# Macaron block on one core: a later state's product ahead of the product with C, softmax steps one at a time, four B/C buffers

## The chip, the cores and the metric

One core of one Trainium2 chip. The metric is the device time of one execution in microseconds (us). Shown are the median of three runs and one profiled execution.

## The reference, cut to what matters

The input is 4 sequences of 1024 rows by 128 features. Three blocks follow each other, each on a layer-normed input and with a residual:

- **Expert block**, used twice, scaled by 0.5: 8 experts, `silu(x @ w_gate[e]) * (x @ w_up[e])` (128 to 512), then `@ w_down[e]` (512 to 128). The experts are summed with weights `cw`: a softmax over 8 router logits times a softmax over 8 gating logits divided by 0.1, divided by its own sum.
- **Mamba block** between them: `x @ W_in` gives `xs` and `z` of 256 channels each; a causal convolution of 4 taps and silu give `xc`; `xc @ W_x` gives 64 rows for `dt` and 16 rows each of B and C. For each of 16 states n: `h = exp(dt*A[n]) * h + (dt*xc) * B[n]`, a scan over 1024 steps, and `y += h * C[n]`. Then `y + D*xc`, times `silu(z)`, `@ W_out`.

## The kernel before, in words

The work is cut into tiles of 512 rows, 8 tiles in all. A tile goes once through the first expert block (kind 0), through mamba, and once through the second expert block (kind 1). The 16 expert passes are *positions*, in the order of `ORDER` (line 35); the last is tile 7 of kind 1. A position has 32 *slots*, one for each expert and group of 128 hidden columns. In each slot TensorE makes six matmuls for gate and up (line 643, 644, 646) and four for the down product (L700, eight records); ScalarE takes the silu of the gate (L1016); VectorE multiplies it by up (L825, the step `first`). After the fourth slot of an expert VectorE weighs the expert's output (L818, step `acc`) and GpSimd's queue adds it to the tile in memory by an accumulating DMA (L1120).

Mamba's states run beside that. For each tile and state n there are: a load of the B and C rows, broadcast to all partitions, into one of `BR` = 3 buffers BCB (L620, SyncE's queue); the product with B, step `s_b` (L912); two scans, `s_scan` j = 0 and 1 (L923); the product with C, step `s_hc` (L931, in place in one of `HR` = 4 buffers HS); two accumulating DMAs Y<-HS (L1137, GpSimd's queue). Each of these DMAs waits until the one of the state before has landed. ScalarE makes the decays (L1085). A tile is closed by `s_yz` (L945, VectorE), `s_out` (L730, TensorE) and `s_add` (L950, VectorE). Then its layer norm can start: ScalarE (L974, L982), GpSimd (L1106 to L1110), ScalarE (L988), four transposes on TensorE (L658), the high and low parts XH (L996 ScalarE, L883 VectorE), and the logits (L666).

The softmax of a position runs on VectorE in ten small instructions, each needing the one before: four (L775, L777, L779, L781; step `p_max`), then the exponentials on ScalarE (L1009, L1010), then six (L786 to L800; steps `p_norm`, `p_sum`, `p_cw`).

**The order of all instructions is made by a planner**, `timetable()` (lines 53 to 422). It is one list of steps; each engine runs its own steps of that list in order and waits on semaphores. The planner keeps a clock for each engine ("pe", "v", "a", "p"), adds a written cost for each step, and lets *streams* (prep, tail, before, scans, closing) give out steps between slots. `side()` gives the streams a turn, three times in a slot; a stream that yields True goes on at once, one that yields False waits for its next turn. `fill(at)` gives out scan steps while VectorE's clock is under a mark 3 us ahead of TensorE's, less 1.0. `finish(k)` drives a stream to its end and adds 0.3 us to TensorE's clock each time round, giving out no slot; it is called for the softmax (`prep`) before the first `acc` of a position, at the position's slot 5. At slot `LATE` = 26 of a position the planner waits in the same way, where the tile of the next position has not yet left mamba. The next position's inputs are forced by slot 29. A state's steps come from `scans(t)` (lines 256 to 290).

The written costs of VectorE's steps are the planner's only knowledge of durations: 1.17 for `s_b` and `s_hc`, 1.22 for a scan, 0.61 for a `first`, 1.0 + 0.4 + 0.3 + 0.35 for the softmax.

Of the kernel before, what the change touches and what calls it, by code (L numbers as in the profile page):

```python
# [20 lines left out]
NS = 16  # L21
# [6 lines left out]
NG = AHEAD + 1  # L28
NB = 4 - NG
HR = 4  # L30
BR = 3
EPS_LN = 1e-5
EPS_CW = 1e-9

# [2 lines left out]
ENDS = (0, NPOS - 1)  # L37
# [15 lines left out]
def timetable():  # L53
# [2 lines left out]


    steps = []
    clock = {"pe": 0.0, "v": 0.0, "a": 0.0, "p": 0.0}
    free = [(0.0, b, None) for b in range(NB)]  # L60

    def step(*what, after=0.0, **work):

        steps.append(what)
        for e, c in work.items():
            clock[e] = max(clock[e], after) + c
            after = clock[e] + SIGNAL[e]
        return after
# [5 lines left out]
    def until(at):  # L74
        while clock["pe"] < at:
            yield False

    def until_v(at):
        while max(clock["v"], clock["pe"]) < at:
            yield False  # L80
# [18 lines left out]
    def norm(b, what):  # L99
        while ln["lock"]:  # L100
            yield False
        ln["lock"] = True
        q = norms[0]
        norms[0] += 1
        yield from rows_of_x()
        yield from calm()
        if q == 0:
            at = step("ln_first", b, what, after=4.0, v=1.5, p=1.2)
            yield "first"
            at = step("ln_first_x", b, after=at, v=.7, a=.9)  # L110
        else:
            at = step("ln_sum", q, b, xn["by"], what, after=clock["pe"], a=1.6)
            yield True
            yield from calm()
            at = step("ln_square", q, b, after=at, a=1.6, p=2.0)
            yield from until(at + .3)
            at = step("ln_x", q, b, after=at, a=1.5)
        ln["lock"] = False
        yield from until(at + 0.7)
        bk = yield from take()  # L120
        at = step("ln_t", q, bk, pe=.6)
        xn.update(by=("m_tr", q + 1), lock=False)
        return q, bk[0], at

    def prep(p):
        kind, t = ORDER[p]
        q, b, at = yield from norm(t % XR, ("x", t) if kind == 0 else ("x2", t))
        at = step("p_xh", p, q, b, after=at, a=.52)
        yield from until_v(at + LATEST)
        at = step("p_xl", p, b, after=at, v=.61)  # L130
        give(b, "v_xl", p + 1, at)
        inputs.add(p)
        yield "inputs"
        yield from until(at)
        bk = yield from take()
        at = step("p_logits", p, bk, pe=.55, a=1.2)
        give(bk[0], "a_lr", p + 1, at)
        yield "logits"
        yield from until_v(at)
        at = step("p_max", p, bk[0], after=at, v=1.0)  # L140
        yield True
        if p == 0:
            yield from until(at + FIRST)
        yield from calm()
        at = step("p_exp", p, after=at, a=3.0)
        yield from until_v(at)
        at = step("p_norm", p, after=at, v=.4)
        yield True
        step("p_sum", p, v=.3)
        yield True  # L150
        step("p_cw", p, v=.35)

    def weigh(g):
        if g % E < E - 1 or g // E not in ENDS:
# [101 lines left out]
    def scans(t):  # L256
        def enter(n):
            step("s_b", t, n, v=1.17)

        bc_loads(t * NS + BR)  # L260
        for n in range(2):
            enter(n)
            yield True
        for n in range(NS):
            m = t * NS + n
            if decayed[0] <= m:
                decays(must=True)
            for j in range(2):
                at = step("s_scan", t, n, j, after=decay_at[m], v=1.22)
                yield True  # L270
            done[0] = m + 1
            decays()
            while t not in begun_y:
                yield False
            at = step("s_hc", t, n, v=1.17)
            if t % 2 == 0 and n:
                step("s_car", t, n - 1, a=.2)
            bc_loads(m + 1 + BR)
            for j in range(2):
                if m < NT * NS - LAST:  # L280
                    clock["p"] = max(clock["p"], at, y_at[j]) + .9
                    y_at[j] = clock["p"] + 5.5
            passed[0] = n
            yield True
            if n + 2 < NS:
                enter(n + 2)
                yield True
        if t % 2 == 0:
            step("s_car", t, NS - 1, a=.2)
        scanned[t] = y_at[1]  # L290
# [79 lines left out]
    for i in range(AHEAD):  # L370
        at = step("first_g", i, pe=.69)
# [4 lines left out]
    for i in range(total):  # L376
        p, r = divmod(i, SLOTS)
        if i + AHEAD < total:
            at = step("first_g", i + AHEAD, after=sil_at.get(i + AHEAD - NG, 0.0), pe=.69)
# [3 lines left out]
        at = step("first", i, after=h_at.get(i - 2, 0.0), pe=.69)  # L383
# [23 lines left out]
        if p + 1 < NPOS and r >= (PREP if p != 1 else LATER) and p + 1 not in prepared:  # L407
            kind, t = ORDER[p + 1]
# [28 lines left out]
def macaron_program(nc, x, W_in, conv_w, conv_b, W_x, W_dt, b_dt, A_log, D_param, W_out,  # L437
# [5 lines left out]
    with ExitStack() as ctx:  # L443
# [21 lines left out]
        LT = sb("LT", [P, SUB, 32])  # L465
# [16 lines left out]
        sm = sb("sm", [P, SUB])  # L482
# [3 lines left out]
        BC = XN[:, :, :].rearrange("p j d -> p (j d)")  # L486
        BCB = sb("BCB", [P, BR, 2, T])
        XS = sb("XS", [P, 2, 2, T + 4])
# [10 lines left out]
        S = {}  # L499
        for n in ("c_small c_con c_wr c_acc c_y0 c_y1 c_bcd c_dt o_x init w_hi w_lo dv "  # L500
# [4 lines left out]
            S[n] = ctx.enter_context(nc.semaphore(n))  # L505
        for b in range(BR):
            S[f"c_bc{b}"] = ctx.enter_context(nc.semaphore(f"c_bc{b}"))
# [63 lines left out]
        def _(sy):  # L571
# [23 lines left out]
            for s in steps:  # L595
# [18 lines left out]
                elif s[0] == "bc_load":  # L614
                    m = s[1]
                    t, n = divmod(m, NS)
                    wt.wait_ge(S["c_bcd"], 16 * (t + 1))
                    if m >= BR:
                        wt.wait_ge(S["v_hc"], m - BR + 1)
                    sy.dma_start(BCB[:, m % BR, :, :], BCD[t % 2, :, n:n + 1, :].rearrange("k n l -> n k l").broadcast_to([P, 2, T])  # L620
# [114 lines left out]
        def _(v):  # L735
            wt = Waits(v)
            v.memset(mhalf[:, :], -0.5).then_inc(S["init"], 1)
            v.memset(DA[:, :, :, T], 1.0).then_inc(S["init"], 1)
            v.memset(DX[:, :, :, T], 0.0).then_inc(S["init"], 1)
            dv = 0  # L740

            def own(z):

                nonlocal dv
                z.then_inc(S["dv"], 1)
                dv += 1

            for s in steps:
                k = s[0]
                if k == "ln_first":  # L750
                    _, b, what = s
# [10 lines left out]
                elif k == "ln_first_x":  # L762
                    b = s[1]
# [4 lines left out]
                    for j in range(2, SUB):  # L768
                        z = v.tensor_scalar(XN[:, j, :], XT[:, b, j, :], rs[:, j:j + 1], nm[:, j:j + 1], ALU.mult, ALU.add)
                    z.then_inc(S["v_xn"], 1)  # L770
                elif k == "p_max":
                    _, p, b = s
                    l4 = LT[:, :, 0:16].rearrange("p j (g e) -> p j g e", g=2)
                    wt.wait_ge(S["a_lr"], p + 1)
                    v.transpose(LT[:, :, :].rearrange("p j r -> p (j r)"), LR[:, :]).then_inc(S["v_lt"], 1)  # L775
                    wt.wait_ge(S["v_lt"], p + 1)
                    own(v.tensor_tensor(LT[:, :, 0:16], LT[:, :, 0:16], LT[:, :, 16:32], ALU.add))  # L777
                    wt.wait_ge(S["dv"], dv)
                    own(v.tensor_reduce(mx[:, :, :], l4, AX.X, ALU.max))  # L779
                    wt.wait_ge(S["dv"], dv)  # L780
                    v.tensor_tensor(lg[:, :, 0:2, :], l4, mx[:, :, :].unsqueeze(3).broadcast_to([P, SUB, 2, E]),  # L781
                                    ALU.subtract).then_inc(S["v_sub"], 1)
                elif k == "p_norm":
                    p = s[1]
                    wt.wait_ge(S["a_exp"], p + 1)
                    own(v.tensor_tensor(lg[:, :, 2, :], lg[:, :, 0, :], lg[:, :, 1, :], ALU.mult))  # L786
                    wt.wait_ge(S["dv"], dv)
                    own(v.tensor_reduce(zz[:, :, :], lg[:, :, :, :], AX.X, ALU.add))
                elif k == "p_sum":
                    wt.wait_ge(S["dv"], dv)  # L790
                    own(v.scalar_tensor_tensor(out=sm[:, :], in0=zz[:, :, 0], scalar=EPS_CW, in1=zz[:, :, 1], op0=ALU.mult,
                                               op1=ALU.mult))
                    wt.wait_ge(S["dv"], dv)
                    own(v.tensor_tensor(sm[:, :], sm[:, :], zz[:, :, 2], ALU.add))
                elif k == "p_cw":
                    p = s[1]
                    wt.wait_ge(S["dv"], dv)
                    own(v.reciprocal(sm[:, :], sm[:, :]))
                    wt.wait_ge(S["dv"], dv)
                    v.scalar_tensor_tensor(out=CW[:, p % 2, :, :], in0=lg[:, :, 2, :], scalar=0.5,  # L800
                                               in1=sm[:, :].unsqueeze(2).broadcast_to([P, SUB, E]), op0=ALU.mult, op1=ALU.mult).then_inc(S["v_cw"], 1)
                elif k == "acc":
                    g = s[1]
                    p, e = divmod(g, E)
# [9 lines left out]
                    else:  # L814
                        n = added(p, e)
# [10 lines left out]
                elif k == "w_split":  # L826
                    e = s[1]
# [23 lines left out]
                elif k == "b_xl":  # L851
                    _, t, q, b = s
# [11 lines left out]
                elif k == "b_halo":  # L864
                    t = s[1]
# [3 lines left out]
                elif k == "b_conv":  # L869
                    _, t, q, j = s  # L870
# [7 lines left out]
                elif k == "p_xl":  # L878
                    _, p, b = s
# [4 lines left out]
                elif k == "b_dx":  # L884
                    t = s[1]
# [10 lines left out]
                elif k == "b_dtl":  # L896
                    _, t, b = s
                    wt.wait_ge(S["a_dbl"], 2 * t + 2)
                    v.tensor_tensor(DTI[RT:2 * RT, :], bank(b)[0:RT, :], f32(DTI[0:RT, :]), ALU.subtract).then_inc(S["v_bc"], 1)
                elif k == "s_b":  # L900
                    _, t, n = s
# [12 lines left out]
                elif k == "s_scan":  # L914
                    _, t, n, j = s
# [9 lines left out]
                elif k == "s_hc":  # L925
                    _, t, n = s
# [5 lines left out]
                elif k == "s_yz":  # L932
                    t = s[1]
# [12 lines left out]
                elif k == "s_add":  # L946
                    _, t, b = s
# [217 lines left out]
```

## Time and profile before

| | |
|---|---|
| median of 3 runs | 1272.25 us (1271.98 to 1272.68) |
| span of the profiled execution | 1272.6 us; no other time of this execution is given |
| TensorE busy | 1253.2 us (98%) |
| VectorE busy | 1114.1 us (88%), little of it idle between 130 and 1172 us |
| ScalarE, GpSimd busy | 926.6 us (73%), 394.3 us (31%) |
| DMA, mean | 144 GB/s |

Read it so: TensorE's busy time counts pipelined matmuls and hides short delays, so the starts of its instructions are to be read too. The scans run from 135 to 1171 us; before and after them VectorE has little to do. A row of the timeline gives the start, the duration, engine, line and operation, and in brackets the engine's idle time before it and what ended it.

### The profile page before, as it was taken

Reading aid. Unit: us, or ns where it says so; the run is one execution under the profiler, and the core shown is the slowest. Engines: PE = TensorE matmul, PEld = TensorE weight load, DVE = VectorE, ACT = ScalarE, POOL = GpSimd, SP = SyncE. Lnnn points to the kernel's source line nnn. Section 1 sums busy time; section 2 is a strip of 40 time slices with the busy share of each in tenths; the row PEclk is TensorE's granted clock in tenths of the full one; section 3 lists DMA queues with packets and bytes.
Section 4 is the critical chain, followed back from the end, with each engine's and each line's share of the span. In section 5 each row is a group of like instructions: output and inputs, shape, how many; then the busy total and the mean of one; then the engine's idle time right before and its main releaser. Section 6 shows DMA issues by size and latency. Waiting matters only on the chain.

```text
span 1272.6 us, 21027 instructions
## 1 busy us (share of the span) xinstructions
PE 1253.2 (98%) x7584; PEld 1096.0 (86%) x7584; DVE 1114.1 (88%) x1481; ACT 926.6 (73%) x1778; POOL 394.3 (31%) x459
## 2 busy tenths in 40 slices
PE   7999999999999999999999999999999999999998
PEld 5888888888888888888888888888888888888887
DVE  4544899989999999999999999999999989999433
ACT  5645978978886978877968788798867968654421
POOL 0101333334342423343333433333334333332110
PEclk9999999999999999999999999999999999999999
DMA  8211677777788868787987878887978887895111
GB/s 244 52 26 30 146 155 154 147 154 158 152 180 164 170 132 183 159 165 161 180 177 150 166 164 176 158 168 148 186 157 167 163 165 142 163 183 107 35 33 33
DMA packets 109303, 182.96 MB, mean 144 GB/s; under 512 B 11024, under 2 KB 23824, under 8 KB 109200
## 3 DMA queue, kind: packets, MB, share of 16 engines
q0 software_dynamic: 56336, 102.79, 45.9%
q1 hardware_dynamic: 52864, 78.85, 24.7%
q8 instruction: 59, 0.97, 0.3%
q14 instruction: 44, 0.36, 0.1%
HBM read 76.22 MB, written 2.62 MB: 62 GB/s over the span
## 4 chain that ended last, share of the span: by engine, by line
PE 73%; DVE 8%; DMA 8%; issue 5%; ACT 3%; POOL 2%; SPq 0%; DVEq 0%; POOLq 0%; ACTq 0%
PE PS L700 27%; PE PS L643 14%; PE PS L646 14%; PE PS L644 14%; DMA Y<-HS 5%; DVE HB L825 2%; DVE HS L923 2%; DMA XS<-DX 2%; DVE HS L931 1%; PE PS L730 1%; PE PS L715 1%; DVE HS L912 1%; PE PS L658 1%; POOL Y L1137 1%; DVE YE L818 1%
## 5 line engine op out<-in xcount | busy, mean ns | idle before, releaser
L700 PEld LDWEIGHTS PS<-WD,HB 128*128 128x128 f32 x4096 | 536.6, 191 | 44.0 <-issue 1.5
L700 PE MATMUL PS<-WD,HB 128*128 128x128 f32 x4096 | 540.1, 275 | 0.0
L1016 ACT ACTIVATE HB<-PS 128x512 f32<-128x512 f32 x512 | 294.3, 596 | 272.9 <-PE PS L646 270.8
L825 DVE TENSOR_TENSOR HB<-PS,HB 128x512 f32<-128x512 f32 x512 | 348.7, 682 | 119.2 <-PE PS L646 110.9
L1137 POOL DMA_DIRECT2D Y<-HS x252 | 221.1, 972 | 383.7 <-DVE HS L931 262.7
L1120 POOL DMA_DIRECT2D XT<-YE x126 | 117.9, 936 | 433.2 <-DVE YE L818 407.4
L643 PE MATMUL PS<-XH,WG 128*128 128x512 f32 x512 | 244.5, 478 | 3.3 <-ACT XH L996 2.3
L643 PE MATMUL PS<-XH,WU 128*128 128x512 f32 x512 | 204.9, 400 | 0.0
L646 PE MATMUL PS<-XH,WG 128*128 128x512 f32 x512 | 203.2, 397 | 0.6 <-DVE XH L883 0.6
L646 PE MATMUL PS<-XH,WU 128*128 128x512 f32 x512 | 202.1, 395 | 0.0
L644 PE MATMUL PS<-XH,WG 128*128 128x512 f32 x512 | 201.0, 393 | 0.0
L644 PE MATMUL PS<-XH,WU 128*128 128x512 f32 x512 | 200.4, 391 | 0.0
L1085 ACT ACTIVATE DA<-XS,aneg 128x512 f32<-128x512 f32 x256 | 164.4, 713 | 1.7 <-DVE HS L923 0.9
L923 DVE TENSOR_TENSOR_SCAN HS<-DA,car,HS 128x512 f32<-128x512 f32 x128 | 162.6, 1277 | 0.0
L931 DVE TENSOR_TENSOR HS<-BCB,HS 128x1024 f32<-128x1024 f32 x128 | 156.2, 1220 | 1.2
L912 DVE TENSOR_TENSOR HS<-BCB,DX 128x1026 f32<-128x1026 f32 (+1 forms) x128 | 155.7, 1220 | 0.1
L923 DVE TENSOR_TENSOR_SCAN HS<-DA,HS 128x513 f32<-128x513 f32 x128 | 154.7, 1219 | 0.0
L646 PEld LDWEIGHTS PS<-XH,WG 128*128 128x128 f32 x512 | 96.5, 188 | 23.9 <-DVE XH L883 1.6
L644 PEld LDWEIGHTS PS<-XH,WU 128*128 128x128 f32 x512 | 96.8, 189 | 23.5 <-issue 1.0
L643 PEld LDWEIGHTS PS<-XH,WU 128*128 128x128 f32 x512 | 96.3, 188 | 23.0 <-issue 1.3
L646 PEld LDWEIGHTS PS<-XH,WU 128*128 128x128 f32 x512 | 96.1, 188 | 23.2
L1016 ACT ACT_TABLE_LOAD x89 | 114.2, 1283 | 2.0 <-PE PS L646 0.3
(109 smaller groups left out, 1080.9 us busy)
## 6 DMA issues: line engine op xcount, KB each, us to landing
BCB<-BCD SPq DMA_DIRECT2D x128, 512.0 KB, 5.3
Y<-HS POOLq DMA_DIRECT2D x252, 256.0 KB, 6.4
XT<-YE POOLq DMA_DIRECT2D x126, 256.0 KB, 4.4
XS<-DX POOLq DMA_DIRECT2D x7, 512.0 KB, 9.2
XT<-in_L_attn_x_dram SPq DMA_DIRECT2D x8, 256.0 KB, 6.5
WD<-in_L_ffn_w_down_dram SPq DMA_DIRECT2D x8, 256.0 KB, 4.8
out_dram<-XT SPq DMA_DIRECT2D x8, 256.0 KB, 5.6
HS<-in_L_ffn_w_gate_dram SPq DMA_DIRECT2D x6, 256.0 KB, 4.0
```

Source lines behind the costliest of these rows:

```text
L643: pe.matmul(o, w[0], m[0], start=True, stop=False)
L644: pe.matmul(o, w[1], m[0], start=False, stop=False)
L646: pe.matmul(o, w[0], m[1], start=False, stop=True).then_inc(S[sem], 1)
L700: z = pe.matmul(expert(g)[:, j, :], HB[:, i % NH, j * P:(j + 1) * P], WD[:, e, c, :], start=c == 0 and j == 0, stop=c == FC - 1 and j == S ...
L825: v.tensor_tensor(H, up(i), H, ALU.mult).then_inc(S["v_h"], 1)
L912: v.tensor_tensor(HS[:, m % HR, :, 0:w], rows.unsqueeze(1).broadcast_to([P, 2, w]), DX[:, t % 2, :, 0:w], ALU.mult).then_inc(S["v_db"], 1)
L923: v.tensor_tensor_scan(H, DA[:, m % NA, j, 0:w], H, car[:, j, n:n + 1] if t % 2 else 0.0, ALU.mult, ALU.add).then_inc(S["v_sc"], 1)
L931: v.tensor_tensor(H, BCB[:, m % BR, 1, :].unsqueeze(1).broadcast_to([P, 2, T]), H, ALU.mult).then_inc(S["v_hc"], 1)
L1016: a.activation(HB[:, i % NH, :], gate(i), ACT.Silu).then_inc(S["a_sil"], 1)
L1085: z = a.activation(DA[:, m % NA, j, 0:T], XS[:, t % 2, j, 3:3 + T], ACT.Exp, scale=aneg[:, j, n:n + 1])
L1120: gp.dma_start(XT[:, ORDER[p][1] % XR, :, :], YE[:, n % 2, :, :], accum_op=ALU.add).then_inc(S["c_acc"], 16)
L1137: gp.dma_start(Y[:, t % 2, j, :], HS[:, m % HR, j, 0:T], accum_op=ALU.add).then_inc(S[f"c_y{j}"], 16)
```

## The change

- The planner notes the last step that had a cost on VectorE (`latest`). `first` is given out without such a cost, so it is not noted.
- If the second scan of state n is the last such step when its product with C is due, the product with B of state n+2 is given out ahead of it (not for n = 14, 15).
- The softmax is cut into ten steps. After each of them, except in the first and last positions, the stream waits until another noted step has been given out, at most six turns (`apart`). The written costs are now .3, .2, .2, .2 and six times .2.
- BCB has 4 buffers in place of 3.

VectorE's instructions and semaphores stay the same otherwise.

```diff
-BR = 3
+BR = 4
...
     def step(*what, after=0.0, **work):
         steps.append(what)
+        if "v" in work:
+            latest[0] = what
...
-        at = step("p_max", p, bk[0], after=at, v=1.0)
+        for what, v in (("p_turn", .3), ("p_fold", .2), ("p_top", .2), ("p_less", .2)):
+            at = step(what, p, after=at, v=v)
+            yield from apart(p)
...
         yield from until_v(at)
-        at = step("p_norm", p, after=at, v=.4)
-        yield True
-        step("p_sum", p, v=.3)
-        yield True
-        step("p_cw", p, v=.35)
+        for what in ("p_both", "p_sums", "p_eps", "p_total", "p_inverse", "p_cw"):
+            at = step(what, p, after=at, v=.2)
+            yield from apart(p)
+
+    def apart(p):
+        mine, tries = latest[0], 0
+        while p not in ENDS and latest[0] is mine and tries < 6:
+            tries += 1
+            yield False
...
             while t not in begun_y:
                 yield False
+            ahead = n + 2 < NS and latest[0] == ("s_scan", t, n, 1)
+            if ahead:
+                enter(n + 2)
+                yield True
             at = step("s_hc", t, n, v=1.17)
...
-            if n + 2 < NS:
+            if n + 2 < NS and not ahead:
                 enter(n + 2)
                 yield True
```

The rest of the diff only splits the branches of VectorE's program so that each of the ten softmax instructions has a step of its own.

## Rows read from the trace of the kernel before

**Rows 1.** The page's busy time, share and instructions of each engine.
```profile
PE 1253.2 (98%) x7584; PEld 1096.0 (86%) x7584; DVE 1114.1 (88%) x1481; ACT 926.6 (73%) x1778; POOL 394.3 (31%) x459
```

**Rows 2.** TensorE's waits: line waited for, us in total, times, longest.
```profile
PE PS L643 <- ACT XH L996: 2.3, 3, 0.8
...
PE PS L730 <- DVE Y L945: 1.3, 2, 1.0
PE PS L646 <- DVE XH L883: 0.6, 1, 0.6
```

**Rows 3.** Busy time of each engine in two stretches, clock, DMA share, GB/s.
```profile
130.00:1172.00 1042.00, 1037.58 (x6305) 908.43 (x6304) 1006.89 (x1279) 822.11 (x1562) 370.83 (x425) 1.00 0.81 161
1172.00:1188.00 16.00, 14.35 (x95) 12.65 (x94) 9.29 (x13) 8.03 (x27) 3.21 (x5) 1.00 0.10 18
```

**Rows 4.** The page's costliest groups, two of VectorE's.
```profile
L825 DVE TENSOR_TENSOR HB<-PS,HB 128x512 f32<-128x512 f32 x512 | 348.7, 682 | 119.2 <-PE PS L646 110.9
...
L931 DVE TENSOR_TENSOR HS<-BCB,HS 128x1024 f32<-128x1024 f32 x128 | 156.2, 1220 | 1.2
```

**Rows 5.** Timeline of VectorE: a scan and the product with C behind it.
```profile
600.99 1.28 DVE L923 TENSOR_TENSOR_SCAN HS<-DA,car,HS 128x512 f32<-128x512 f32 x1
602.31 1.23 DVE L931 TENSOR_TENSOR HS<-BCB,HS 128x1024 f32<-128x1024 f32 x1
```

**Rows 6.** Timeline of VectorE: softmax of position 2, and its first weighing.
```profile
168.97 0.30 DVE L775 STREAM_TRANSPOSE LT<-LR 128x128 f32<-128x128 f32 x1
169.30 0.23 DVE L777 TENSOR_TENSOR LT<-LT 128x64 f32<-128x64 f32 x1
...
173.42 0.18 DVE L786 TENSOR_TENSOR lg<-lg 128x32 f32<-128x32 f32 x1
...
174.53 0.19 DVE L800 SCALAR_TENSOR_TENSOR CW<-lg,sm 128x32 f32<-128x32 f32 x1
174.64 0.68 DVE L818 TENSOR_TENSOR YE<-PS,CW 128x512 f32<-128x512 f32 x1
...
182.75 0.69 DVE L818 TENSOR_TENSOR YE<-PS,CW 128x512 f32<-128x512 f32 x1
```

**Rows 7.** Timeline of VectorE and TensorE: the longest stretch without an L825.
```profile
227.72 0.68 DVE L825 TENSOR_TENSOR HB<-PS,HB 128x512 f32<-128x512 f32 x1
...
228.32 2.33 DVE L923 TENSOR_TENSOR_SCAN HS<-DA,HS 128x513 f32<-128x513 f32 x2
...
233.89 1.29 DVE L825 TENSOR_TENSOR HB<-PS,HB 128x512 f32<-128x512 f32 x2
233.94 0.48 PE L643 MATMUL PS<-XH,WG 128*128 128x512 f32 x1
```

**Rows 8.** Timeline of TensorE where the last position begins.
```profile
1176.79 1.95 PE L730 MATMUL PS<-WO,Y 128*128 128x128 f32 x16
...
1183.06 0.48 PE L643 MATMUL PS<-XH,WG 128*128 128x512 f32 x1
...
1186.55 0.63 PE L658 MATMUL PS<-CON,XN 128*128 128x128 f32 x4 [0.97 <-ACT XN L988]
...
1194.75 0.48 PE L643 MATMUL PS<-XH,WG 128*128 128x512 f32 x1
...
1197.04 0.48 PE L643 MATMUL PS<-XH,WG 128*128 128x512 f32 x1
```

**Rows 9.** Timeline where tile 3 is closed: GpSimd, VectorE, TensorE.
```profile
661.71 0.86 POOL L1137 DMA_DIRECT2D Y<-HS  x1 [0.32 <-DMA Y<-HS]
...
667.67 1.23 DVE L945 TENSOR_TENSOR Y<-Y,SZ 128x1024 f32<-128x1024 f32 x1 [1.62 <-DMA Y<-HS]
...
669.05 1.13 PE L730 MATMUL PS<-WO,Y 128*128 128x128 f32 x8 [0.35 <-DVE Y L945]
```

**Rows 10.** What touches BCB: count, duration min/median/max ns, first and last start.
```profile
L931 DVE TENSOR_TENSOR HS<-BCB,HS x128: 1211/1219/1227, 141.6 to 1169.9; 128x1024 f32<-128x1024 f32 x128
```

**Rows 11.** The page's DMA issues: queue, count, size of one, median us to landing.
```profile
BCB<-BCD SPq DMA_DIRECT2D x128, 512.0 KB, 5.3
```

More of the change, by code:

```diff
@@ L58, in timetable @@
     steps = []
+    latest = [None]
     clock = {"pe": 0.0, "v": 0.0, "a": 0.0, "p": 0.0}
@@ L740, in _ @@
             dv = 0
+            l4 = LT[:, :, 0:16].rearrange("p j (g e) -> p j g e", g=2)
             def own(z):
@@ L770, in _ @@
                     z.then_inc(S["v_xn"], 1)
-                elif k == "p_max":
-                    _, p, b = s
-                    l4 = LT[:, :, 0:16].rearrange("p j (g e) -> p j g e", g=2)
+                elif k == "p_turn":
+                    p = s[1]
                     wt.wait_ge(S["a_lr"], p + 1)
                     v.transpose(LT[:, :, :].rearrange("p j r -> p (j r)"), LR[:, :]).then_inc(S["v_lt"], 1)
-                    wt.wait_ge(S["v_lt"], p + 1)
+                elif k == "p_fold":
+                    wt.wait_ge(S["v_lt"], s[1] + 1)
                     own(v.tensor_tensor(LT[:, :, 0:16], LT[:, :, 0:16], LT[:, :, 16:32], ALU.add))
+                elif k == "p_top":
                     wt.wait_ge(S["dv"], dv)
                     own(v.tensor_reduce(mx[:, :, :], l4, AX.X, ALU.max))
+                elif k == "p_less":
                     wt.wait_ge(S["dv"], dv)
@@ L782, in _ @@
                                     ALU.subtract).then_inc(S["v_sub"], 1)
-                elif k == "p_norm":
+                elif k == "p_both":
                     p = s[1]
@@ L786, in _ @@
                     own(v.tensor_tensor(lg[:, :, 2, :], lg[:, :, 0, :], lg[:, :, 1, :], ALU.mult))
+                elif k == "p_sums":
                     wt.wait_ge(S["dv"], dv)
                     own(v.tensor_reduce(zz[:, :, :], lg[:, :, :, :], AX.X, ALU.add))
-                elif k == "p_sum":
+                elif k == "p_eps":
                     wt.wait_ge(S["dv"], dv)
@@ L792, in _ @@
                                                op1=ALU.mult))
+                elif k == "p_total":
                     wt.wait_ge(S["dv"], dv)
                     own(v.tensor_tensor(sm[:, :], sm[:, :], zz[:, :, 2], ALU.add))
+                elif k == "p_inverse":
+                    wt.wait_ge(S["dv"], dv)
+                    own(v.reciprocal(sm[:, :], sm[:, :]))
                 elif k == "p_cw":
                     p = s[1]
-                    wt.wait_ge(S["dv"], dv)
-                    own(v.reciprocal(sm[:, :], sm[:, :]))
                     wt.wait_ge(S["dv"], dv)
```

## The prediction

> **What bounds the kernel now.** I read the page's busy times first. TensorE is busy 98% of the span, VectorE 88% [rows 1]. All that TensorE does is the same work after the change, so only its idle time can be won. I then cut the span where the scans end. From 130 to 1172 us TensorE lacks 4.4 us of 1042.0 and VectorE 35.1; in the 16 us behind it TensorE lacks 1.65 [rows 3]. In the same long stretch VectorE is 97% busy, so two engines run close to full there, and TensorE is the one that sets the end.
>
> Next, TensorE's own waits. Those that VectorE ends come to 1.3 + 0.6 = 1.9 us; those on ScalarE's XH to 2.3 [rows 2]. No row has TensorE waiting for L825. VectorE, on the other hand, is idle 110.9 us before L825 for TensorE's matmuls [rows 4], most of it outside the scans, where all of its idle time is only the 35.1 us. So a shorter VectorE instruction sequence by itself buys little. What the change can do is move the **place** of work in the order.
>
> The largest single loss is where the last position begins. Two starts of a gate matmul one slot apart are 1197.04 - 1194.75 = 2.29 us apart, and 1183.06 to 1194.75 is three slots, so 6.87 us in place of 11.69 [rows 8]. Of the 4.8 us over, four transposes and two logits matmuls are work that stays: at most the 0.63 of the transposes' row and as much again, so 3.6 to 4.8 us are lost; I take 4.0. The cause is an order that is too late: tile 7's L730 starts at 1176.79, its transposes can start only at 1186.55, after the layer norm, and by then TensorE has used up what could go before. If L730 stood two slots (4.6 us) earlier, all of the loss would go.
>
> **The change part by part.**
>
> *Dependent neighbours.* An instruction that needs the one before it starts just after its end: 602.31 against 600.99 + 1.28 = 602.27, so +0.04; 169.30 against 168.97 + 0.30, so +0.03 [rows 5, 6]. One that doesn't starts before that end: 174.64 against 174.53 + 0.19 = 174.72, so -0.08 [rows 6]. A pair pulled apart saves 0.11 to 0.13 us; I take 0.12. The softmax has 3 + 5 = 8 such pairs in a position, and 14 positions are changed: 112 x 0.12 = 13.4 us. Of scan and product with C, 35 of 128 pairs are such neighbours (the one shown is one of them): at most 35 x 0.12 = 4.2 us. In 57 more states only an L825 stands between, which is not noted by the planner, so the products swap places there and nothing is saved. Sum: 17.6 us of VectorE's time at most. On the path this is worth between 0 and the 1.9 us that TensorE waits for VectorE. One of the two waits (L883) comes from ScalarE's XH first, and the other from a DMA [rows 9], so I take 0.5 us, nearer to nothing.
>
> Here the Trainium skill speaks against the change. VectorE: DVE Perf Modes, section "The DRAIN you can't avoid", says that a semaphore between chained instructions costs nothing extra, as the pipe is emptied in any case, and its rules say to reduce the number of instructions, not of semaphores. By it the 17.6 us would be nothing and the sum below 0.5 us higher. The two kinds of start above differ by 0.12 us, so this trace disagrees.
>
> *Written costs.* The softmax is planned at 0.9 + 1.2 = 2.1 us instead of 2.05. Over 15 positions before the scans end that is 0.75 us more, a third of a slot. The planner does not learn of the 17.6 us: VectorE's order is as dense as before and VectorE waits a bit more for TensorE.
>
> *The softmax takes longer.* A slot of 2.29 us holds one L825 (0.68 less the 0.09 by which starts overlap, 0.59) and so 1.70 us of other VectorE work. A softmax step with a scan-type step behind it is about 0.15 + 1.13 = 1.28 us (L931's 1.22 less 0.09 [rows 4]), so 1.33 pairs fit in a slot, and ten steps take 7.5 slots or 17 us. The wait for the exponentials adds 3.4 us: the first four steps are over about 1.0 us after 168.97, and L786 starts at 173.42 [rows 6]. In most positions the softmax starts around slot 14 to 23 of the position before and has 14 slots or more: no cost. Position 2 is different. Its softmax starts at 168.97 and its first weighing stands at 182.75 [rows 6], 13.8 us later, where 20.6 are wanted. So `finish` is called with some 5 steps left and drives them through: about five pairs, 6.4 us, are put between two L825s, with an L818 and the L825 itself 7.6 us. The longest such stretch now is 233.89 - 227.72 = 6.17 us, and TensorE starts its next gate at 233.94 with no idle time shown [rows 7]. The cost is thus from 0 (as in that stretch) to 7.6 - 2.29 = 5.3 us (nothing hides it). I take what goes over the stretch that was borne, 7.6 - 6.2 = 1.4 us.
>
> *What that does to the order.* In `finish` TensorE's planned clock runs on without giving out slots, and VectorE's list gets 6.4 us of scan work ahead of its slots. Scans are planned without gaps from there to the end, so they end 6.4 / 2.29 = 2.8 slots earlier, less a third for the written costs: 2.5 slots. Then L730 of tile 7 and the last layer norm stand more than two slots earlier, and the 4.0 us go. The real VectorE can keep to that: it has 35.1 us idle in the scans and 17.6 more. If only 3 us are pushed through, it is one slot, and 2.3 of the 4.0 go.
>
> *The product with C later.* It slides by one L912, 1.13 us, in some 80 of 128 states (those with only L825s between, n = 14 and 15 left out). Queued behind it are GpSimd's two DMAs Y<-HS and, behind those, the layer norm's small instructions and the expert additions on the same queue. In mid-tile the buffer HS has two states' time, about 16 us of (1169.9 - 141.6) / 127 = 8.1 each [rows 10], less 2.3 for both moves: covered. At a tile's end it is not: at tile 3 VectorE sits idle 1.62 us until Y<-HS lands and TensorE 0.35 us until L945 is through [rows 9]. State 13's late product pushes the chain of landings by up to 1.1 us. I count four tile ends as tight: 0 to 4.4 us. The planner carries that delay in its clock and moves L730 back with it, so I take 0.4.
>
> *Four buffers.* SyncE's load of a later state goes out one state (8.1 us) sooner against a product with B 1.13 us sooner, landing in 5.3 us [rows 11]. No bytes more. With three buffers the move would eat into the load's lead; with four it costs nothing. A load put ahead could slow the Y<-HS landings; DMA share is 0.81 [rows 3]. Nothing taken.
>
> **Sum** against the execution's 1272.6 us: -4.0 + 1.4 + 0.4 - 0.5 = -2.7, so 1269.9. The median of the runs stands 0.35 lower: **1269.6 us**.
>
> **Rivals.**
>
> - *Only reshuffled.* The push at position 2 is small, or later places give it back, and the end stall stays. For: the loss at the end depends on one slot's place; other small TensorE waits (XH, 2.3 us) fall anew. Against: nothing in the order absorbs work from the scans. Time 1272, within 2.5 of before.
> - *The stretch at position 2 is not borne*: 5.3 us, and the gain at the end stays away because the pushed work is on VectorE before it has caught up. Place: TensorE about 185 us. Decides once VectorE's stretch between two L825s exceeds 6.2 us. Time 1272.3 + 5.3 = 1277.6 without the gain, 1273.6 with it.
> - *Tile ends.* State 13's product is late and L730, in a fixed place, waits: up to 4 x 1.1 = 4.4 us, 1276.7. Decides where Y<-HS lands after the planned place of L945. For: 1.62 and 0.35 us idle there already. Against: the planner counts the move.
> - *It doesn't separate.* Six tries run out, or the pushed steps stand side by side. Then VectorE saves less than 17.6 us; the time is that of the reshuffle.
>
> **Chances.** Measurements of this kernel spread by 0.7 us; 0.2%, 2.5 us, is about what can be told from no change. Forecast (end stall gone, 1267 to 1269.8): 0.42. Reshuffled: 0.35. Slower: 0.23, of it 0.12 for the stretch and 0.11 for tile ends. The best case, end stall and the 1.9 + 2.3 us of rows 2 gone, is 1264; I put the low end at 1266.5 and the high at 1276.5, which leaves a tenth outside on each side. The forecast's own range is 1267 to 1271.
>
> **What would show it.** The step in TensorE's starts at the last position falls from 4.0 us to under 1; L730 of tile 7 stands at least two slots earlier before the last position's first gate. VectorE's gap behind a softmax step is -0.08, not +0.03, and L912 stands ahead of L931 in some 80 states. VectorE idles more before L825 in the scans. Position 2 has a stretch of 6 to 8 us without L825 at 180 to 190 us. I am wrong if the last position begins with the same step, if TensorE waits for L825's output anywhere, or if L730's waits grow beyond 1.3 us.

## The result, and the profile after

The changed kernel takes **1277.98 us** (median of 5 runs, 1276.56 to 1279.02) against 1272.25 (1271.13 to 1274.63): ratio **1.0046**, 95% interval 1.0033 to 1.0059. It is slower by 5.7 us, where 2.7 us faster was forecast, and outside the range of 1266.5 to 1276.5. All times below are medians; one of the first experiment's eleven executions was a slow one (1389.79 us at a mean granted clock of 0.852) and is not in its ratio.

The profiled execution of the changed kernel has a span of 1275.0 us. The one of before has 1272.6, and that difference of 2.4 us is smaller than the medians'. The order of before was profiled once more, with four buffers (below, ratio 0.9991), and there the span is 1269.0: TensorE's granted clock stayed at 1.00 where the last position begins, while it was 0.72 from 1187 to 1192 us in the execution shown before, and TensorE waits nowhere for L945 (1.3 us before). Spans of single executions are therefore compared with care. The experiments were timed later, each beside fresh executions of the kernel before (medians of 1271.9 to 1272.3), so a difference of two medians and that of their ratios can be up to 1 us apart; where that matters, both are given.

In the changed program the lines have moved: L825 is now L844, L912 L931, L923 L942, L931 L950, L818 L837, L945 L964, L730 L743, L658 L671, L643/L644/L646 are L656/L657/L659, L988 is L1007, L996 L1015.

The page's busy times of the changed kernel, against [rows 1]:

```profile
PE 1252.9 (98%) x7584; PEld 1096.1 (86%) x7584; DVE 1105.2 (87%) x1481; ACT 927.2 (73%) x1778; POOL 389.7 (31%) x459
```

The stretches of [rows 3] and the place of the loss in the changed kernel (columns as there: span, then busy time of PE, PEld, DVE, ACT, POOL, then TensorE's clock, DMA share, GB/s):

```profile
130.00:1172.00 1042.00, 1034.81 (x6280) 906.34 (x6279) 995.60 (x1276) 821.63 (x1560) 366.15 (x425) 1.00 0.80 161
...
186.00:196.00 10.00, 5.46 (x34) 4.44 (x33) 9.05 (x11) 7.73 (x27) 6.96 (x9) 0.99 0.75 161
196.00:200.00 4.00, 4.00 (x19) 3.44 (x17) 2.47 (x4) 2.53 (x12) 1.29 (x2) 0.61 1.01 196
```

VectorE did become shorter. Over the whole execution its same 1481 instructions take 1105.2 us in place of 1114.1: 8.9 us less. (The stretch above shows 11.3 us less, 1006.89 to 995.60, but it ends at a fixed time and holds 3 instructions fewer of a kernel that is behind.) TensorE lost 2.8 us more in the scans, and one place holds more than that: from 186 to 196 us it is busy 5.46 of 10 us (10.00 before). For the 4 us behind that idle time the granted clock is 0.61, mostly the lower of its two levels, 1.2 in place of 2.4 GHz, at which matmuls start 0.43 us apart in place of 0.23.

TensorE's waits of the changed kernel, against [rows 2]:

```profile
PE PS L671 <- ACT XN L1007: 4.3, 3, 3.4
PE PS L656 <- ACT XH L1015: 2.2, 3, 0.8
PE PS L656 <- ACT HB L1035: 1.5, 1, 1.5
PE PS L656 <- DVE HB L844: 1.1, 1, 1.1
```

Two are new: a wait of 3.4 us for a layer norm's output, and one of 1.1 us for L844, VectorE's product in the expert block, which TensorE never waited for before. The waits for L945 (1.3 us) are gone, but so they are in the order of before when it was profiled again.

VectorE in the timeline of the changed kernel, where position 2's softmax is driven to its end, against [rows 6, 7]:

```profile
181.36 0.69 DVE L844 TENSOR_TENSOR HB<-PS,HB 128x512 f32<-128x512 f32 x1
181.97 0.16 DVE L808 SCALAR_TENSOR_TENSOR sm<-zz 128x4 f32<-128x4 f32 x1
182.04 1.22 DVE L942 TENSOR_TENSOR_SCAN HS<-DA,HS 128x513 f32<-128x513 f32 x1
183.17 0.14 DVE L812 TENSOR_TENSOR sm<-sm,zz 128x4 f32<-128x4 f32 x1
183.23 1.22 DVE L942 TENSOR_TENSOR_SCAN HS<-DA,HS 128x513 f32<-128x513 f32 x1
184.36 0.15 DVE L815 RECIPROCAL sm<-sm 128x4 f32<-128x4 f32 x1
184.49 1.22 DVE L950 TENSOR_TENSOR HS<-BCB,HS 128x1024 f32<-128x1024 f32 x1
185.63 0.18 DVE L819 SCALAR_TENSOR_TENSOR CW<-lg,sm 128x32 f32<-128x32 f32 x1
185.73 1.22 DVE L931 TENSOR_TENSOR HS<-BCB,DX 128x1026 f32<-128x1026 f32 x1
186.87 0.68 DVE L837 TENSOR_TENSOR YE<-PS,CW 128x512 f32<-128x512 f32 x1
187.47 0.68 DVE L844 TENSOR_TENSOR HB<-PS,HB 128x512 f32<-128x512 f32 x1
```

Four softmax steps, each with a mamba step behind it, stand between two L844s, 187.47 - 181.36 = 6.11 us apart. An instruction that does not need the one before it starts ahead of its end (183.17 + 0.14 = 183.31, next start 183.23). And TensorE just behind:

```profile
188.20 0.50 PE L656 MATMUL PS<-XH,WU 128*128 128x512 f32 x1 [1.14 <-DVE HB L844]
...
191.28 1.05 PE L713 MATMUL PS<-WD,HB 128*128 128x128 f32 x8
195.73 1.09 PE L671 MATMUL PS<-CON,XN 128*128 128x128 f32 x4 [3.40 <-ACT XN L1007]
196.47 0.78 PE L656 MATMUL PS<-XH,WG 128*128 128x512 f32 x1
...
1180.00 1.95 PE L743 MATMUL PS<-WO,Y 128*128 128x128 f32 x16
...
1190.48 0.63 PE L671 MATMUL PS<-CON,XN 128*128 128x128 f32 x4 [0.78 <-ACT XN L1007]
```

First 1.14 us for L844, then 3.40 us for the fifth layer norm's output, then the slow matmuls. Counted by starts of the same slots against the re-profiled order of before, the changed kernel is 0.2 us behind when position 2 begins, 4.9 when position 4 does and 6.0 at the end. (At the start of position 10 it is 7.9, but of that 1.8 us are an L743 that stands four slots earlier in the changed order; when the order of before has had its own, 6.1 are left.) The last two rows are those of [rows 8]: the last L743 and the transposes behind it stand where they stood in the order, L743 at slot 26 of position 14.

### The profile page after: what moved, and what is told of

It is laid out like the page before. It is cut to its first block, busy times and chain, and to the rows that moved or that the text cites. A ratio compares the mean times of both kernels' runs of the same rounds, so it can differ in the third digit from the quotient of the medians.

```text
span 1275.0 us, 21026 instructions
## 1 busy us (share of the span) xinstructions
PE 1252.9 (98%) x7584; PEld 1096.1 (86%) x7584; DVE 1105.2 (87%) x1481; ACT 927.2 (73%) x1778; POOL 389.7 (31%) x459
## 4 chain that ended last, share of the span: by engine, by line
PE 94%; ACT 4%; issue 1%; DVE 1%; DMA 0%; POOL 0%; SPq 0%; DVEq 0%; ACTq 0%; POOLq 0%
PE PS L713 34%; PE PS L656 19%; PE PS L659 19%; PE PS L657 18%; PE PS L743 1%; PE PS L728 1%; PE PS L671 1%; ACT DA L1104 1%; ACT HB L1035 1%; PE PS L679 1%; ACT L1035 1%; ACT XN L1007 0%; ACT L1104 0%; PE PS L735 0%; ACT XN L1001 0%
## 5 line engine op out<-in xcount | busy, mean ns | idle before, releaser
L844 DVE TENSOR_TENSOR HB<-PS,HB 128x512 f32<-128x512 f32 x512 | 348.0, 680 | 126.4 <-PE PS L659 115.8
L656 PE MATMUL PS<-XH,WG 128*128 128x512 f32 x512 | 244.6, 478 | 4.4 <-ACT XH L1015 2.2
L656 PE MATMUL PS<-XH,WU 128*128 128x512 f32 x512 | 205.2, 401 | 1.1 <-DVE HB L844 1.1
L659 PE MATMUL PS<-XH,WG 128*128 128x512 f32 x512 | 203.6, 398 | 0.0
L659 PE MATMUL PS<-XH,WU 128*128 128x512 f32 x512 | 202.0, 394 | 0.0
L657 PE MATMUL PS<-XH,WG 128*128 128x512 f32 x512 | 201.1, 393 | 0.0
L657 PE MATMUL PS<-XH,WU 128*128 128x512 f32 x512 | 200.5, 392 | 0.0
L942 DVE TENSOR_TENSOR_SCAN HS<-DA,car,HS 128x512 f32<-128x512 f32 x128 | 162.4, 1274 | 0.0
L950 DVE TENSOR_TENSOR HS<-BCB,HS 128x1024 f32<-128x1024 f32 x128 | 155.6, 1215 | 0.1
L931 DVE TENSOR_TENSOR HS<-BCB,DX 128x1026 f32<-128x1026 f32 (+1 forms) x128 | 155.2, 1216 | 0.0
L942 DVE TENSOR_TENSOR_SCAN HS<-DA,HS 128x513 f32<-128x513 f32 x128 | 154.7, 1217 | 0.0
L656 PEld LDWEIGHTS PS<-XH,WU 128*128 128x128 f32 x512 | 96.3, 188 | 24.4 <-DVE HB L844 2.2
L657 PEld LDWEIGHTS PS<-XH,WU 128*128 128x128 f32 x512 | 96.8, 189 | 23.4 <-issue 1.0
L659 PEld LDWEIGHTS PS<-XH,WG 128*128 128x128 f32 x512 | 96.6, 189 | 23.3 <-DVE XH L902 1.0
L659 PEld LDWEIGHTS PS<-XH,WU 128*128 128x128 f32 x512 | 96.1, 188 | 23.1
```

What stands on the lines that cost most here:

```text
L656: pe.matmul(o, w[0], m[0], start=True, stop=False)
L657: pe.matmul(o, w[1], m[0], start=False, stop=False)
L659: pe.matmul(o, w[0], m[1], start=False, stop=True).then_inc(S[sem], 1)
L844: v.tensor_tensor(H, up(i), H, ALU.mult).then_inc(S["v_h"], 1)
L931: v.tensor_tensor(HS[:, m % HR, :, 0:w], rows.unsqueeze(1).broadcast_to([P, 2, w]), DX[:, t % 2, :, 0:w], ALU.mult).then_inc(S["v_db"], 1)
L942: v.tensor_tensor_scan(H, DA[:, m % NA, j, 0:w], H, car[:, j, n:n + 1] if t % 2 else 0.0, ALU.mult, ALU.add).then_inc(S["v_sc"], 1)
```

## The experiments

The changed kernel and the experiments were timed against the kernel before; all ratios are to it.

**Position 2's softmax together.** The changed kernel with

```diff
-        while p not in ENDS and latest[0] is mine and tries < 6:
+        while p not in ENDS + (2,) and latest[0] is mine and tries < 6:
```

> The changed kernel, but position 2's ten softmax steps stand together as in the first and last positions. Theory A (position 2 is the place of the loss: its softmax, one step at a time, is not done when the first weighing is due, the planner drives it through, VectorE's stretch without L825 grows to 6.1 us and the planner's TensorE clock runs 4.8 us ahead, so that the next layer norm's transposes stand too early): the 1.1 us and 3.4 us of TensorE's idle time between 187 and 197 us go, ratio to before 0.999 to 1.001, about 1272. Theory B (the products with C, late by one instruction in some 100 states, cost through the Y<-HS landings and the tile ends): they are all still here, so it stays at 1277 to 1278, ratio 1.004 to 1.005. Theory C (a new order costs wherever it falls, no one place): anything between, 1274 to 1276.

1270.13 us, ratio 0.9990 (0.998 to 1.0), 7.9 us less than the changed kernel (7.1 by the ratios), and 2 us less than the expectation had it. Its stretch around position 2's first weighing, beside that of the changed kernel above:

```profile
186.00:200.00 14.00, 14.00 (x90) 12.39 (x89) 13.12 (x17) 13.34 (x36) 5.77 (x7) 1.00 0.81 166
1172.00:1188.00 16.00, 14.37 (x91) 12.17 (x91) 7.53 (x14) 9.65 (x32) 3.22 (x5) 1.00 0.20 35
```

TensorE is busy for all 14 us. The rest of the change is not slower than before. The last position still begins with its loss, 14.37 of 16 us.

**Position 2 alone.** The order of before, four buffers, and only position 2's softmax one step at a time (the other positions' steps together at the old written costs, no product moved). As an edit of the changed kernel:

```diff
+        if p == 2:
             for what, v in (("p_turn", .3), ("p_fold", .2), ("p_top", .2), ("p_less", .2)):
                 at = step(what, p, after=at, v=v)
                 yield from apart(p)
+        else:
+            for what in ("p_turn", "p_fold", "p_top"):
+                steps.append((what, p))
+            at = step("p_less", p, after=at, v=1.0)
... (the last six steps in the same way)
-            ahead = n + 2 < NS and latest[0] == ("s_scan", t, n, 1)
+            ahead = False
```

> The order of the kernel before, with four buffers, in which position 2 alone has its softmax one step at a time; no product with B is moved ahead and all other softmaxes stand together. Theory A: all of the loss is here, 1277 to 1279, ratio 1.004 to 1.006, with TensorE idle 4 to 5 us between 185 and 200 us. Theories B and C: one position's ten small instructions can't do it, 1272 to 1273, ratio under 1.001.

1282.97 us, ratio 1.009 (1.0075 to 1.0105): one position's ten small instructions make it 11 us slower, more than the whole change does. TensorE's rows around position 2's first weighing, in its timeline:

```profile
189.97 0.50 PE L671 MATMUL PS<-XH,WU 128*128 128x512 f32 x1 [1.91 <-DVE HB L859]
195.78 0.65 PE L686 MATMUL PS<-CON,XN 128*128 128x128 f32 x4 [3.96 <-ACT XN L1022]
```

The same two waits, both longer. (Here L859 is the expert product, L686 the transposes.) What drives them is larger too: VectorE's stretch between two L859s is 189.24 - 182.02 = 7.22 us, and the planner's TensorE clock runs 5.7 us ahead in place of 4.8. The loss is larger than the 1277 to 1279 expected; besides these 5.9 us there are smaller new waits at later places (1.5 us for a closing product, 0.5 us for the expert product).

**The swap alone.** The kernel before with the product with B two states on ahead of the product with C, and four buffers; softmax as before.

```diff
-BR = 3
+BR = 4
...
+            ahead = n + 2 < NS and latest[0] == ("s_scan", t, n, 1)
+            if ahead:
+                enter(n + 2)
+                yield True
             at = step("s_hc", t, n, v=1.17)
...
-            if n + 2 < NS:
+            if n + 2 < NS and not ahead:
```

> The kernel before with the product with B of two states later ahead of the product with C, and four buffers; the softmax as before. Theory A: no loss, 1271.5 to 1273. Theory B: the loss is here, 1276 to 1278. Of VectorE's dependent neighbours scan and product with C some 35 go, 4 us of VectorE's time, and the total moves by under 1 us for it.

1274.0 us, ratio 1.0018 (1.0009 to 1.0027): 2 us slower, between the two expectations and nearer to the first. The new waits are four of TensorE between 516 and 541 us (1.33, 1.13, 0.61 and 0.59 us), for the silu twice, the layer norm and the expert product; the one for a closing product is 1.1 us (1.3 in two waits before). So the swap by itself costs a little in this order, and why that one group of waits falls as it does was not followed further.

**The changed kernel without the swap**

```diff
-            ahead = n + 2 < NS and latest[0] == ("s_scan", t, n, 1)
+            ahead = False
```

> The changed kernel without the swap: the product with B of two states later stays behind the product with C everywhere, the softmax steps stand apart, four buffers. Position 2 is driven through by 5.7 us of the planner's clock here (4.8 with the swap). Theory A: at least as slow as the changed kernel, 1278 to 1283 (like position 2 alone, 1283, in which the push is 5.7 too). Theory B (the swap costs): faster than the changed kernel by 2 us or more, 1272 to 1276.

1279.78 us, ratio 1.0059 (1.0047 to 1.0071). Slower still, with waits of 1.91 and 3.95 us at position 2. The swap is not the cause. That it helps isn't shown either: without it the planner's clock runs 5.7 us ahead at position 2 in place of 4.8.

**Four buffers alone**

```diff
-BR = 3
+BR = 4
```

> The kernel before with four B/C buffers in place of three and nothing else. Product with B never waited for its load before, so under every theory 1271.5 to 1273, ratio 0.999 to 1.001. Were it slower by 0.2% or more, the loads that go out earlier would disturb the Y<-HS landings, and part of the loss of the swap alone (ratio 1.0018) would be theirs.

1271.62 us, ratio 0.9991 (0.9982 to 1.0). No cost. By the ratio it gains about 1 us, and the interval reaches no gain at all.

**The transposes later, by two amounts.** The changed kernel; position 2 is still driven through. The fifth layer norm's transposes (q = 4) are due later on the planner's TensorE clock:

```diff
-        yield from until(at + 0.7)
+        yield from until(at + 0.7 + (3.5 if q == 4 else 0.0))
```

> The changed kernel with one edit: the fifth layer norm's transposes (the one behind which TensorE sat idle 3.4 us at position 2) are due 3.5 us later on the planner's TensorE clock, as much as that clock ran ahead. Position 2's softmax is still driven through. Theory A with two parts: the part by the early transposes (3.4 us idle and the slower matmuls behind it, 4 to 5 us) goes, the part by VectorE's 6.1 us stretch (1.1 us idle) stays; 1273 to 1275. In this order the last L730 also moves from slot 26 to 24, so up to 3 us less: 1271 to 1275. If VectorE's long stretch is what costs, nothing goes: 1277 to 1278.

1269.44 us, ratio **0.9983** (0.9974 to 0.9991). It was 8.5 us faster than the changed kernel (8.0 by the ratios), more than the 3 to 7 us expected. Then the same with 3.0 for 3.5, where the last L743 keeps slot 26:

> The changed kernel with the fifth layer norm's transposes due 3.0 us later in place of 3.5: they move behind the next gate, and the last L730 stays at slot 26, where it is in the changed kernel. It separates the two parts of the earlier run's gain of 8.5 us. If position 2's transposes are one part and the last position's start the other: some 3 us of the idle time at position 2 go and the loss of 4 us at the last position stays, 1273 to 1275, ratio 1.001 to 1.003. If the gain was all at the last position: 1277 to 1278. If it was all at position 2: 1270.

1273.31 us, ratio 1.0009 (1.0001 to 1.0018). TensorE's rows of this one:

```profile
188.35 0.51 PE L656 MATMUL PS<-XH,WU 128*128 128x512 f32 x1 [1.14 <-DVE HB L844]
...
195.89 0.63 PE L671 MATMUL PS<-CON,XN 128*128 128x128 f32 x4 [0.42 <-ACT XN L1007]
...
1185.70 0.63 PE L671 MATMUL PS<-CON,XN 128*128 128x128 f32 x4 [0.96 <-ACT XN L1007]
1187.02 0.50 PE L656 MATMUL PS<-XH,WG 128*128 128x512 f32 x1 [0.69 <-ACT XH L1015]
```

VectorE's part stays to the hundredth, 1.14 us. The transposes' part falls from 3.40 to 0.42 us, and in the profiled execution the clock stays at 1.00 from 196 to 200 us. The median is 4.7 us below the changed kernel's, of the 5.7 lost. (The profiled execution is the fastest of the twelve, so how much of the 4.7 is wait and how much clock can be read for it alone.) The other 3.9 us of the first edit (3.3 by the ratios) came with an order in which the last L743 stands at slot 24. In its trace the transposes at the last position start at 1183.15 with no wait, and the two slots there take 6.66 us in place of 7.83: 1.2 us. The rest was not traced to a place.

**Lower written costs, position 2 still driven through**

```diff
-        for what, v in (("p_turn", .3), ("p_fold", .2), ("p_top", .2), ("p_less", .2)):
+        for what, v in (("p_turn", .2), ("p_fold", .15), ("p_top", .15), ("p_less", .15)):
...
-            at = step(what, p, after=at, v=.2)
+            at = step(what, p, after=at, v=.1)
```

> The changed kernel with the softmax steps' written costs at .2, .15, .15, .15 and .1 six times (1.25 us in all). The order still drives position 2 through (3.9 us), but the scans are over sooner and the last L730 stands at slot 21 of position 14 in place of 26. This is the order that the prediction had in mind. If an earlier L730 is all that the last position's start needs: its loss of 4.0 us is gone, under 0.5 us of idle time there, and the time is 1277.98 - 4 = 1274, less 1 for the smaller push: 1273. If the real VectorE can't keep up with an order this dense: TensorE waits for L825 or for the closing product in the scans, and the time is 1276 or more.

1270.47 us, ratio 0.9996 (0.9987 to 1.0004). The order has the last L743 at slot 21, and the stretch where the last position begins:

```profile
1172.00:1200.00 28.00, 28.00 (x174) 24.53 (x173) 12.73 (x26) 13.82 (x31) 4.08 (x6) 1.00 0.17 29
```

No idle time is left. In mid-scan one closing product is now late (1.7 us). It is 3 us better than expected. The fifth layer norm's transposes stand at slot 11 of position 2 in this order too, as in the last two (9 in the changed one), and don't wait, which the expectation had not reckoned with.

**Position 2 together and lower written costs, in three strengths.** All have position 2 together. First the softmax at .25, .15, .15, .15 and six times .12:

> As the first of these runs (position 2 together), and the planner's written costs of the softmax steps are brought down to what they take when they stand apart (.25, .15, .15, .15, then .12 six times, 1.42 in place of 2.1 us). If the planner's belief in VectorE's time is what holds the last L730 at slot 26 of position 14: it moves to slot 24, the last position's start loses 2 to 4 us less, 1268 to 1270, ratio 0.997 to 0.999. If the real VectorE can't keep to that order, TensorE waits for L825 in the scans and the time is 1273 or more.

1271.45 us, ratio 1.0001 (0.9991 to 1.0011), where 1268 to 1270 was expected. The last L743 moved to slot 24 as expected, but the loss at the last position fell by 1.1 us and not by 2 to 4 (two slots take 6.68 us in place of 7.83), and TensorE waits 3.3 us for closing products, which it did not with position 2 together and the costs left alone.

```profile
PE PS L743 <- DVE Y L964: 3.3, 2, 2.4
```

Then .15 for the last six softmax steps, scans 1.21, products 1.15:

> Candidate for a version better than both: position 2 together, written costs a little nearer to the trace for all of VectorE's mamba steps (scan 1.21, products 1.15, softmax .3, .2, .2, .2 and .15 six times). The last L730 stands at slot 23. If the only losses left were the one at the last position: 1270.1 - 3 = 1267, ratio 0.996 to 0.998. If VectorE is asked for too much, the closing products wait as in the run with costs down: 1270 to 1272.

1272.09 us, ratio 1.0 (0.9991 to 1.0009), with 3.4 us of the same waits. Last, only

```diff
-            at = step(what, p, after=at, v=.2)
+            at = step(what, p, after=at, v=.16)
```

> Position 2 together and the last six softmax steps written as .16: the last L730 stands at slot 24 of position 14, all else near to the run with position 2 together (1270.1). If nothing in mid-scan turns up, the last position's start loses 1 in place of 4 us: 1267 to 1268, ratio 0.996 to 0.998. If an order two slots denser makes a closing product wait, as with all costs down: 1269 to 1272.

**1267.8 us, ratio 0.9964 (0.9952 to 0.9976)**: 0.4% faster than the kernel before, and faster than the changed one. TensorE's waits in it:

```profile
PE PS L671 <- ACT XN L986: 8.3, 1, 8.3
PE PS L656 <- ACT XH L1015: 2.2, 3, 0.8
PE PS L743 <- DVE Y L964: 0.5, 1, 0.5
PE PS L656 <- DVE WG L851: 0.5, 1, 0.5
```

The first is the start of the kernel. Neither the wait for L844, nor those for L1007 are there. The last L743 stands at slot 24, and at the last position that is worth 1.1 us.

## Why the prediction was wrong, point by point

**Dependent neighbours: the size was nearly right, the worth nearly nothing.** At most 17.6 us of VectorE's time was forecast. In the changed order only 2 products with C stand right behind their scan (35 before), and only 16 softmax neighbours are left, those of the first and last positions; so 33 + 112 = 145 pairs were pulled apart. VectorE's busy time fell by 8.9 us. It does not hold the short pause in front of a dependent instruction: pauses of less than 0.06 us fell from 198, 6.7 us in all, to 51, 1.7 us in all. Together that is 13.9 us, or 0.10 us for each pair where 0.12 was taken. The Trainium skill (VectorE: DVE Perf Modes, "The DRAIN you can't avoid") says that a semaphore between chained instructions costs nothing extra. Taken as the prediction took it, that keeping them apart gives nothing, the trace does not agree: the same 1481 instructions took 8.9 us less of busy time. The time did not reach the end, as foretold, since TensorE sets it.

**The stretch at position 2: right place, right term, a part missing.** The step foresaw that the softmax would not be done by the first weighing, that the planner would drive it through, and a stretch of 7.6 us that costs 1.4 us. Measured: 6.11 us and 1.14 us. The two costs are near each other by luck: the stretch is shorter than the 6.17 us that were borne at another place, [rows 7], so by the prediction's own bound it should have cost nothing. (Why that place bears more was not tested; likely TensorE had more left to do there.) The planner's TensorE clock ran 4.8 us ahead (6.4 were foreseen), and this was counted as a gain only. It is also a shift of everything that the planner places by that clock. The fifth layer norm's transposes were put in TensorE's list as if ScalarE had had 4.8 us more: four slots behind the layer norm's first step (slots 5 and 9 of position 2), where before they stand five behind it (9 and 14) and with position 2 alone three (5 and 8, and a wait of 3.96 us). TensorE, which takes its list in order, waited 3.40 us for their input, and its clock fell for 4 us. (ScalarE was not what was full: its L1007 starts at 193.94, after 2.21 us in which ScalarE was idle for a result of GpSimd's.) The edit of this one place gave back 4.7 us with VectorE's stretch still there. This is most of the loss, and the sum had no term for it: the first step that failed.

**The end stall: the other step that failed.** "Scans are planned without gaps from there to the end, so they end ... 2.5 slots earlier" turned into the term of -4.0, and the gain was 0. In the changed kernel the closing L743s of tiles 0 to 4 do stand 3, 5, 2, 3 and 4 slots earlier, that of tile 6 three, and those of tiles 5 and 7 stand at the slots of before. The scans are not without gaps. VectorE between tile 6's last product with C and tile 7's first product with B, in the changed kernel:

```profile
1041.56 1.22 DVE L950 TENSOR_TENSOR HS<-BCB,HS 128x1024 f32<-128x1024 f32 x1
...
1054.99 1.22 DVE L914 TENSOR_TENSOR DX<-XS,Y 128x1024 f32<-128x1024 f32 x1
...
1056.73 2.36 DVE L931 TENSOR_TENSOR HS<-BCB,DX 128x1024 f32<-128x1024 f32 x2
```

The product with C ends at 1042.78, so for 13.95 us there is no scan work; the next product with B needs L914, which makes tile 7's input. In the execution before the same gap is 9.67 us (1043.32 to 1052.99). Counted by the slots of the L844s, tile 6's last product stands two slots earlier than before, tile 7's first one slot, and tile 7's L743 again at slot 26. So the lead is used up in front of the next tile's input, and nothing was won at the end. By the code a tile's input is made only when its pass through the first expert block is over, and that pass is bound to its slots and not to the scans; that this is what holds it was not tried apart.

Tile 5 lost its lead in another way. Its closing product was done early, and its matmuls waited for their turn in TensorE's list:

```profile
920.91 1.23 DVE L964 TENSOR_TENSOR Y<-Y,SZ 128x1024 f32<-128x1024 f32 x1 [2.21 <-DMA Y<-HS]
...
931.39 0.79 PE L743 MATMUL PS<-WO,Y 128*128 128x128 f32 x5
```

They come 10.5 us after L964 (the row ends where the view does, after 5 of 16), behind another layer norm's transposes at 921.53 and its logits at 926.84. By the code all three take the one spare PSUM bank of the planner (`take`), which is a likely reason; it was not tried apart either.

That an earlier one removes the loss is shown: at slot 21 TensorE is busy for 28.00 of 28.00 us. The size was also too large: in the order of before, profiled again, the two slots in question (1180.99 to 1188.81 us) take 7.8 us, less two of 2.29 and some 0.8 of real work (the prediction's figure): 2.4 us are lost. In the changed kernel they take 7.65 us, so the loss is as good as whole. The other 1.6 us of the 4.0 were the lower clock of that one execution.

With the two steps put right the sum is -2.7 + 4.0 + 4.7 = 6.0 us, and 5.7 were measured.

**The tile ends** cost nothing: TensorE's waits for the closing product are none, against 1.3 us before and none in the order of before profiled again, so the change can't be credited with it. The swap was made in 61 states, not some 80, since other steps stand between scan and product more often in the new order. Without the swap the kernel is slower, not faster; alone it costs 2 us, at other places. Waits for the B/C loads did not come, as foretold.

**The rivals.** The second rival (the stretch at position 2 not borne, 1277.6) came out within 0.4 us of the result, but by another way: it priced VectorE's stretch at 5.3 us, which is 1.14 us, and the rest is the transposes. That it is so near is luck.

**The marks.** "Position 2 has a stretch of 6 to 8 us" came true, and so did the gap behind a softmax step (-0.08 us above) and more idle time of VectorE before the expert product (126.4 us, 119.2 before). L931 stands ahead of L950 in 61 states and not some 80, and tile 7's L743 did not move. "TensorE waits for L825's output" came true and the step at the last position stayed: these two were to prove the forecast wrong. The spread of 0.7 us that the chances rest on comes from three executions; the five of the result spread over 3.5 us.

## What to carry to other kernels

A planner that drives a stream to its end by advancing one engine's clock without giving that engine work shifts all that it later places by this clock, on engines that have nothing to do with the stream. Before splitting a short chain into steps with pauses, find the place with the least time between its start and its deadline, and leave the chain whole there: here this turned 0.5% slower into no difference from before (ratio 0.9990, interval up to 1.0). And when instructions have become shorter, tell the planner a little of it, not all: .16 for .2 us gave 0.3% more, in one order that was tried, while lower costs made closing products late in two. And before a lead is carried to the end of a plan, look in each gap of the stream for what it waits for: here the next tile's input took the lead back.

## What the runs showed of the hardware that was not expected

A wait of 3.40 us of TensorE was followed by a granted clock of 0.61 over the next 4 us, which cost about 1.6 us on top: six matmuls took 2.69 us from start to start (196.47 to 199.16) in place of 1.47, and the four transposes 0.74 in place of 0.38. Waits of 1.14 and 0.42 us, 7 us apart, at the same place were not followed by a lower clock in the profiled execution of the second transposes run. At the last position the same order of instructions, with waits of 0.97 and 0.69 us, had the clock at 0.72 in one execution and at 1.00 in another, and the same three slots took 11.69 and 10.11 us. So single executions of one order differ by some 1.6 us from this alone.

The mean clock of a whole execution shows it too. Of the twelve executions of the second transposes run the three at 0.997 took 1275.3 to 1275.6 us and the three at 1.000 took 1271.8 to 1272.7. In the first transposes run all eleven had 1.000, and they lie within 1.2 us.
